# Two transformer layers on one core: where GpSimd pauses, who makes the token weights, and in which order blocks and copies are issued between the router and the expert tiles

## The reference

```python
logits = _gelu(x @ rw1) @ rw2                 # router, 8 experts
probs = jax.nn.softmax(logits, axis=-1)
wgt, idx = jax.lax.top_k(probs, TOP_K)        # TOP_K = 2
for e in range(E):
    Ye = _gelu(x @ w1[e] + b1[e]) @ w2[e] + b2[e]
    Ce = _gelu(b1[e]) @ w2[e] + b2[e]
    for k in range(TOP_K):
        mask = idx[..., k] == e
        active = jnp.any(mask).astype(x.dtype)
        out = out + active * wgt[..., k:k + 1] * jnp.where(mask[..., None], Ye, Ce)
```

## Time and profile before

| what | value |
|---|---|
| three timed runs | 407.2, 411.9, 412.66 us; median 411.9 us |
| the profiled execution | 405.77 us, of which its span is 403.9 us |
| TensorE matmul busy | 315.3 us, 78% of the span |
| VectorE busy | 306.2 us, 76% |
| ScalarE busy | 267.8 us, 66% |
| GpSimd busy | 180.6 us, 45% |
| mean granted TensorE clock | 0.925 of full speed |

### The profile page before, as it was taken

How to read it: one execution, slowest core, us unless ns; L and a number is a source line. 1 busy time by engine, 2 the same in 40 slices (tenths; PEclk the granted TensorE clock), 3 DMA queues, 4 the chain that set the end, 5 groups by cost and what they waited for, 6 DMA issues and landing times.

```text
span 403.9 us, 8728 instructions
## 1 busy us (share of the span) xinstructions
PE 315.3 (78%) x2708; PEld 217.7 (54%) x2709; DVE 306.2 (76%) x745; ACT 267.8 (66%) x540; POOL 180.6 (45%) x245
## 2 busy tenths in 40 slices
PE   0075988989989996878767215798999999999991
PEld 0053327655467654545434114665777777777760
DVE  4998998793875566897989885784787777788760
ACT  1825767634696388889798665661777778777770
POOL 3052305293286058535567459311444455445432
PEclk9998899989999999999979555896999999999997
DMA  5950001943097158431406549445678777777522
GB/s 181 379 238 0 2 0 62 174 110 100 0 148 223 39 71 181 118 108 36 123 15 198 156 108 337 181 178 208 161 247 263 254 230 247 228 218 256 156 27 26
DMA packets 27298, 60.48 MB, mean 150 GB/s; under 512 B 4305, under 2 KB 17954, under 8 KB 24066
## 3 DMA queue, kind: packets, MB, share of 16 engines
q1 hardware_dynamic: 20658, 53.20, 40.5%
q0 software_dynamic: 4416, 6.13, 9.4%
q10 hardware_dynamic: 2192, 0.75, 0.7%
HBM read 29.00 MB, written 6.85 MB: 89 GB/s over the span
## 4 chain that ended last, share of the span: by engine, by line
PE 45%; DVE 29%; ACT 10%; issue 9%; DMA 4%; POOL 1%; ACTq 0%; DVEq 0%; POOLq 0%
PE bank L1270 8%; PE bank L1637 7%; PE bank L1655 7%; PE bank L1640 4%; PE bank L1658 4%; DVE MX L2000 3%; PE bank L1231 2%; DMA STG<-in_l_w_dram 2%; ACT arena L1131 2%; DVE arena L2287 2%; PE bank L1356 2%; DVE stats L1720 2%; PE bank L1382 1%; DVE arena L2292 1%; ACT arena L997 1%
## 5 line engine op out<-in xcount | busy, mean ns | idle before, releaser
L1655 PE MATMUL bank<-arena 128*128 x184 | 63.4, 390 | 2.6 <-DVE X L2274 1.1
L1131 ACT ACTIVATE arena<-arena,B1D 128x128 f32<-128x128 f32 x184 | 57.4, 392 | 8.8 <-DVE arena L2287 8.3
L2287 DVE TENSOR_REDUCE arena<-bank 128x256 f32<-128x512 f32 x92 | 57.3, 681 | 2.5 <-PE bank L1640 2.4
L685 POOL TENSOR_TENSOR W<-STG,W 128x256 f16<-128x256 f32 x64 | 42.7, 700 | 33.2 <-ACT W L882 28.7
L782 POOL DMA_INDIRECT out_dram<-arena,SI x23 | 36.4, 1584 | 36.4 <-DMA out_dram<-arena,SI 19.2
L1658 PE MATMUL bank<-arena 128*128 x184 | 51.2, 279 | 0.0
L685 POOL TENSOR_TENSOR arena<-STG,arena 128x256 f16<-128x256 f32 x56 | 37.5, 705 | 26.4 <-ACT arena L882 24.9
L1637 PE MATMUL bank<-arena 128*128 128x256 f16 x256 | 45.6, 279 | 1.7 <-DVE arena L2250 1.7
L2292 DVE SCALAR_TENSOR_TENSOR arena<-arena 128x512 f16<-128x512 f32 x46 | 29.7, 688 | 22.7 <-ACT arena L1138 22.7
L769 POOL DMA_INDIRECT arena<-token_rows,GI x23 | 22.8, 993 | 51.4 <-ACT WS L1125 43.3
L1640 PE MATMUL bank<-arena 128*128 128x128 f16 x256 | 44.7, 224 | 0.0
(11 more groups left out here) (280 smaller groups left out, 715.1 us busy)
## 6 DMA issues: line engine op xcount, KB each, us to landing
STG<-in_l_w_dram SPq DMA_DIRECT2D x32, 512.0 KB, 4.0
arena<-W SPq DMA_DIRECT2D x16, 1024.0 KB, 4.6
STG<-W SPq DMA_DIRECT2D x7, 1024.0 KB, 5.0
arena<-in_l_w_dram SPq DMA_DIRECT2D x2, 1280.0 KB, 7.3
k_parts<-W SPq DMA_DIRECT2D x2, 768.0 KB, 4.4
arena<-k_parts SPq DMA_DIRECT2D x12, 128.0 KB, 5.2
X<-in_x_dram SPq DMA_DIRECT2D x2, 512.0 KB, 7.4
W<-in_ctx_dram SPq DMA_DIRECT2D x1, 1024.0 KB, 10.2
```

The lines of the kernel that those rows point to most:

```text
L685: ins = nc.gpsimd.tensor_tensor(l, src, h, ALU.subtract)
L1131: ins = nc.scalar.activation(x, x, ACT.Gelu, bias=B1D[:, e, c:c + 1], scale=1.0 / (X_SCALE * W_SCALE))
L1655: nc.tensor.matmul(bank[6 + q][:, :], GDL[:, q, 0, c * P:(c + 1) * P], W2[:, e, c].rearrange("p s d -> p (s d)"), start=(c == 0), stop=Fal ...
L2287: v.tensor_reduce(half, o, AX.X, ALU.add).then_inc(s_dadd, 1)
```

## The change

GpSimd's stretch of low parts for blocks 23 to 25 gets three waits: it goes on only when the first of the last two normalised rows is out (`s_dhs`), after two instructions only when the second router split is done (`s_rhl` 2), after four more only when the third is (`s_rhl` 3). After block 25 it waits for the token weights' scale `RS` and multiplies it out to `DWE` itself; VectorE no longer does. The store of `DWE` gets a semaphore of its own, `s_wrows`, on which only the first gather waits; SP's first `W1` copy waits for the other two stores alone. On ScalarE, scaling block 24 moves ahead of the last `row_high`, the whole of block 25 ahead of the third `router_gelu`, scaling block 26 ahead of the exponentials, and blocks 26's high part and 27 ahead of the store of `DWE`. On SP, the second half of `token_rows` is stored one block load earlier, and the second `W1` copy is issued behind the loads of blocks 30 and 31 instead of ahead of them.

```diff
-            for i in range(25, 28):
+            for i in range(25, 27):
                 load_weights(i)
             store_token_rows(1)
-            for i in range(28, BLOCKS - 2):
+            for i in range(27, BLOCKS - 2):
                 load_weights(i)
...
-            sp.wait_ge(s_rows, 16 * 3)
-            for r in range(2):
-                load_tile_weights(r, r, first=True)
+            sp.wait_ge(s_rows, 32)
+            load_tile_weights(0, 0, first=True)
             for i in range(BLOCKS - 2, BLOCKS):
                 load_weights(i)
+            load_tile_weights(1, 1, first=True)
             sp.wait_ge(s_wlo, BLOCKS - 2)
...
-            def weights_low(i):
+            def weights_low(i, cs=range(HID // D)):
...
-            for i in D_BLOCKS[1:-4]:
+            pool.wait_ge(s_dhs, T - 1)
+            weights_low(D_BLOCKS[1], range(2))
+            pool.wait_ge(s_rhl, 2)
+            weights_low(D_BLOCKS[1], range(2, 4))
+            weights_low(D_BLOCKS[2], range(2))
+            pool.wait_ge(s_rhl, 3)
+            weights_low(D_BLOCKS[2], range(2, 4))
+            weights_low(D_BLOCKS[3])
+            pool.wait_ge(s_dl, 3)
+            nc.gpsimd.tensor_tensor(DWE[:, :, :], PR[:, :, 0:E], RS[:, :].unsqueeze(2).broadcast_to([P, T, E]),
+                                    ALU.mult).then_inc(s_dwe, 1)
+            for i in D_BLOCKS[4:-4]:
                 weights_low(i)
...
-            pool.wait_ge(s_rows, 16 * 3)
+            pool.wait_ge(s_rows, 32)
+            pool.wait_ge(s_wrows, 16)
             pool.wait_ge(s_gi, 1)
...
+            weights_scale(D_BLOCKS[2])
             for t in range(T - 2, T):
                 row_high(t)
-            weights_scale(D_BLOCKS[2])
+            weights_high(D_BLOCKS[2])
             rows_t_out(3)
-            weights_high(D_BLOCKS[2])
-            weights_scale(D_BLOCKS[3])
+            weights_split(D_BLOCKS[3])
             router_gelu(2)
...
+            weights_scale(D_BLOCKS[4])
             act.wait_ge(s_dl, 2)
...
-            weights_high(D_BLOCKS[3])
+            weights_high(D_BLOCKS[4])
+            weights_split(D_BLOCKS[5])
             act.wait_ge(s_dwe, 1)
             act.dma_start(token_rows[:, D:ROW].rearrange("(t p) e -> p t e", p=P),
-                          DWE[:, :, :].bitcast(U32)).then_inc(s_rows, 16)
-            for i in D_BLOCKS[4:-2]:
+                          DWE[:, :, :].bitcast(U32)).then_inc(s_wrows, 16)
+            for i in D_BLOCKS[6:-2]:
                 weights_split(i)
...
-            step(v.tensor_scalar(RS[:, :], DTOPF[:, :, 0], tg[:, 3:4], 1.0 / (G_SCALE * W_SCALE), ALU.mult, ALU.mult))
-            v.tensor_tensor(DWE[:, :, :], PR[:, :, 0:E], RS[:, :].unsqueeze(2).broadcast_to([P, T, E]),
-                            ALU.mult).then_inc(s_dwe, 1)
+            v.tensor_scalar(RS[:, :], DTOPF[:, :, 0], tg[:, 3:4], 1.0 / (G_SCALE * W_SCALE), ALU.mult, ALU.mult
+                            ).then_inc(s_dl, 1)
```

More of the change, by code:

```diff
@@ L409, in flamingo @@
         s_lread = sem("first_router_logits_read")
-        s_dl = sem("router_logits_less_max")
+        s_dl = sem("router_logits_less_max_and_row_scale")
         s_ex = sem("router_exponentials")
@@ L416, in flamingo @@
         s_gbz = sem("gelu_spread_cleared")
-        s_slot = sem("slots_ready")
+        s_wrows = sem("token_weights_stored")
         s_eid = sem("tile_experts_ready")
@@ L676, in _ @@
             estimate_rstd(3, 1)
-            def weights_low(i):
+            def weights_low(i, cs=range(HID // D)):
                 _, hi, lo = weight_block(i)
                 pool.wait_ge(s_whi, i + 1)
-                for c in range(HID // D):
+                for c in cs:
                     src = STG[:, i % 4, c * D:(c + 1) * D]
@@ L685, in weights_low @@
                     ins = nc.gpsimd.tensor_tensor(l, src, h, ALU.subtract)
-                ins.then_inc(s_wlo, 1)
+                if c == HID // D - 1:
+                    ins.then_inc(s_wlo, 1)
             def ones_rows(b):
```

## The result

The changed kernel took 404.2 us in the median of 6 runs (401.71 to 412.36), the kernel before 410.0 in the median of 6 on the same chip: a ratio of 0.9871, 95% interval 0.9825 to 0.9916, so 5.3 us less. (One of the 6 runs, 412.36, lies 2.7% above the fastest and stays out of the ratio.) In the profiled executions it is 401.71 against 405.77 us, spans of 399.9 and 403.9, at a mean granted clock of 0.928 and 0.925.

The account below looks back on a forecast made before the run. Tile 0's start was taken as the bound, set by block 30's load and the gather. An earlier gather landing plus 0.4 from `late_low` gave 4.0 us: 411.9 to 407.9 (span 403.9 to 399.9), range 402.5 to 412.0, chance 0.62.

Parts of the forecast that it names:

- the gather that passes: Rival, chance 0.16: gather passes SP's transfers, landing soon after issue, and tile 0 runs at full clock; gain 7.2, 404.7 us.
- Newton step and third split: VectorE's small instructions no longer slowed beside GpSimd: 1.3 and 0.75 us earlier, less 0.1 lost on ScalarE.
- Token weights' part: VectorE's expert choice: 0.65 saved by moving L2188, 0.6 lost beside GpSimd; `EID` and `GI` 1.9 earlier, bounds 1.4 to 2.5.
- GpSimd's own list: GpSimd's remaining low parts and `DWE` end at 242.6 instead of 246.47, 3.9 us earlier; gather issued at 243.5.
- First copy: SP's first W1 copy, no longer waiting for the weights' store, issued at 240.0 or earlier, 1.9 us sooner.
- Landing of the gather: Tile 0's gather queues behind SP's transfers: lands at 248.0, 249.7 or 251.3; the middle taken, tile 0 3.9 us earlier.
- the last case: At the gather's landing: second W1 copy ahead of the gather, landing at 251.3, tile 0 2.3 us earlier.
- the first case: At the gather's landing: second W1 copy behind the gather, landing at 248.0, tile 0 5.6 us earlier.
- Block 30 out of the way: Block 30 loads behind the first copy only; its ScalarE and VectorE work ends by 249.1, saving 0.4 at tile 0.
- The queue takes it back: Rival, chance 0.16: second copy ahead of the gather, more VectorE waits beside GpSimd; gain 1.4 to 2.3, 410.1 us.
- Slower: Rival, chance 0.06: TensorE's clock stays lower into the tiles, costing 4.8 us over three tiles; 412.7 us.
- The passing case's second half: Within the 0.16 rival of a passing gather: TensorE keeps the clock, so tile 0 goes up 1.6 us faster.

Follow-up runs that it names:

- the repeat: The changed kernel timed once more, nothing altered, beside the kernel with the gather first: median 406.5 us, ratio 0.9886 to the kernel before.
- no_rest: The changed kernel without GpSimd's three waits: ratio 0.9905 to the kernel before.
- rest_only: The kernel before with GpSimd's three waits and nothing else: ratio 0.9983 to the kernel before.
- gather_first: The changed kernel with SP's second W1 copy held back until the first gather has landed: median 401.7 us against 408.5 before, ratio 0.9828.
- the repeats: The changed kernel and the one holding SP's second copy until the gather lands, both timed again on one chip: 406.5 and 404.6 us, ratios 0.9886 and 0.9838.
- copy_only: The kernel before with only the second W1 copy moved behind the loads of blocks 30 and 31: median 407.2 us against 408.5, ratio 0.9866.
- scalar_as_before: The changed kernel with ScalarE's blocks in the order of the kernel before: 403.8 us, read by its events alone.

## Why the prediction was right, and where its steps were off

The time, 404.2, lies in the range, faster by 1.3% where about 1% was forecast. It is 3.7 us under the forecast of 407.9: 1.9 because the kernel before came out at 410.0 in this set and not at 411.9, 1.8 because the medians lie 5.8 apart and not 4.0. It lies nearer the 404.7 of the gather that passes, a case that did not occur, so the time alone would have pointed at the wrong mechanism. The profiled span is the 399.9 us that the sum gave. That agreement is luck: 1.37 of it came ahead of the anchor and 0.49 went again behind tile 0's start. What the passage gave, counted from the anchor, is 30.43 - 27.31 = 3.12 us where the sum has 4.0; the repeat gives 2.78. (The range's ends are 0.2 and 0.1 us off the working given for them, 404.7 - 2 and 410.1 + 2; nothing hangs on it.)

*Newton step and third split*: right. The first of the last two rows began 1.40 after the anchor against 2.72, so 1.32 for 1.3; the third split was done 2.02 earlier, where 1.3 and 0.75 less 0.1 had been counted.

*Token weights' part*: the sign of each piece was right, the sum too careful. L2186 and the cast lost 0.41 and 0.17, together the 0.58 that had been taken as 0.6; but the product (L2201) fell from 0.48 to 0.17, where I had let it stay, since it met GpSimd just ahead of an instruction's end, and the two copies ahead of `GI` went from 1.27 to 0.65, beginning at 240.49 when GpSimd was through its blocks (240.22). The 0.46 that the sum took over from the Newton step was not a fixed price, as the two timelines above show. `EID` came 2.43 earlier instead of 1.9, `GI` 2.77, outside the bound of 2.5. `DWE` on GpSimd took 0.29, at the low end of 0.2 to 0.7.
The Trainium skill, page "SBUF — State Buffer", section "Who interferes with whom", says that an instruction with two SBUF inputs contends with a GpSimd instruction that reads SBUF. The trace agrees for L2186 (0.16 to 0.57), while the subtraction that reads the logits from PSUM beside the same GpSimd work (L2184) stayed at 0.22. The cast, with one SBUF input, and the scale, with one and a column of scalars, were held up too (0.22 to 0.39, and 0.71 against the 0.22 of no_rest).

*GpSimd's own list*: block 27 was done 17.55 after the anchor, where 242.6 is 18.56, 1.0 sooner than taken. The gather was issued where the sum had it (19.52; 243.5 is 19.46), but by luck: `GI` came 0.9 sooner than taken, and 0.95 went between its end and the gather's start, for which the sum had nothing.

*First copy*: mis-sized. It came 2.93 earlier, not 1.9: 0.53 from `EID`, and 0.5 since it had waited 1.44 behind `EID` for the weights' store and now stands 0.94 behind. I had written that the store no longer counts, and put nothing on it. rest_only shows the worth of it: with that wait left in, `EID` earlier by 1.61 moved the copy by 0.96.

*Landing of the gather*, the step that decided: I took the middle of behind, shared and ahead (249.7, that is first copy's issue plus 9.7). It was the last case: issue plus 11.4, as in the kernel before. SP's issue of the second copy began 0.18 us behind the gather's, but the gather's own took 1.22 us, and the copy kept most of the gather's packets back to its end. This step failed by 1.7 us against me; the copy's 1.0 made up part of it, and moving `late_low` out of the way gave 0.2 instead of 0.4. gather_first shows what the first case would have given: tile 0 5.64 earlier than before, and 5.6 had been written for it. Its terms were others: the gather landed 5.67 earlier instead of 5.2, and the 0.4 of `late_low` was not saved, since block 30 was the last wait.

*Block 30 out of the way*: right, 5.6 us earlier on ScalarE, off the chain.

*Rivals.* "The queue takes it back" had the mechanism that ruled, the copy ahead of the gather, at 1.4 to 2.3 us; the passage gave 3.1 since the copy itself came earlier than that sum allowed. "The gather passes" did not occur: the gather landed 6.8 us after its issue, and gather_first shows what held it. "Slower" did not occur either: tile 0 went up at a granted 0.61, as before (0.62), and from 255 to 270 us the clock was 1.00. The passing case's second half, 1.6 us from a tile 0 at full clock (2.4 GHz, against mostly 1.2), was met by chance in gather_first. Busy times by stretch while tile 0 goes up (us; PE, PEld, DVE, ACT, POOL; granted clock; DMA; GB/s), changed kernel, then gather_first:

```profile
249.98:254.17 4.19, 4.19 (x32) 3.45 (x33) 1.84 (x3) 1.90 (x4) 1.74 (x3) 0.61 0.40 130
```

```profile
249.64:252.40 2.76, 2.76 (x34) 2.56 (x35) 1.89 (x3) 1.09 (x1) 2.76 (x6) 1.00 0.85 321
```

The tile went up 1.43 us faster, but from its start to the end of the span only 0.56 of it was left. Counted from tile 0's start, tile 1 went up 1.24 us earlier, but tile 0's way down began only 0.61 earlier: ahead of it TensorE waited 1.34 us for VectorE, against 0.69 in the changed kernel. So more than half of the clock's gain was lost to VectorE there. It is one pair: in the repeats tile 0 took 4.74 and 4.30 us to go up, neither at full clock, and the two rests differ by 0.07.

*What stays open.* The passage gave 3.1 us and, in the repeat, 2.8; the timed ratios give 5.3 and 4.7, with intervals from 3.4 to 7.2 and from 1.7 to 7.6. Both the head ahead of the anchor (222.67 to 229.02 in identical code) and the rest behind tile 0 (147.7 to 150.3) vary by more than that gap. In the rest it goes with a stretch of low granted clock. Stretches with it, kernel before, changed, copy_only (columns as above):

```profile
270.00:285.00 15.00, 13.71 (x86) 8.94 (x83) 9.10 (x19) 4.96 (x14) 2.92 (x3) 0.77 0.50 158
```

```profile
265.00:280.00 15.00, 13.71 (x85) 9.13 (x83) 9.11 (x19) 4.54 (x13) 2.59 (x2) 0.77 0.46 152
```

```profile
270.00:285.00 15.00, 13.71 (x95) 9.46 (x94) 10.19 (x22) 5.70 (x17) 3.58 (x3) 0.89 0.50 159
```

At 0.89 the rest took 147.7, at 0.77 149.4 and 149.9. In copy_only tile 0 went up at full clock besides. scalar_as_before had both as well (0.89 over the same window, 147.9), gather_first the fast tile 0 but 0.77, and took 149.4; so the later stretch is the likelier cause, though no run changes it alone. Whether the change makes the kinder pattern more frequent, or the gap is the noise of few runs, the runs don't tell.

## What to carry to other kernels

Count a small gather's landing from the first transfer that the big queue has outstanding, not from its own issue, and move what isn't needed yet behind it: one wait on SP was worth 2.5 us at tile 0's start here, nearly as much as the whole change (3.1). An earlier result pays only if the wait that stands beside it goes too: resting GpSimd alone brought `EID` forward by 1.6 and tile 0 by 0.4. And compare two traces from an event ahead of the change; here a third of the gain in span had nothing to do with it.

## What the hardware showed that I had not expected

GpSimd began a gather 0.95 us after the end of the row that wrote its indices (241.24 to 242.19), where an instruction queued behind its own list waited 0.19; I had taken the issue to be at the writing. And a gather begun 0.18 us ahead of a 1 MB copy still landed as late as with the copy in front; its own issue lasts 1.22 us. In copy_only and scalar_as_before it began 0.9 us ahead of the copy, still less than that, and landed 10.9 and 12.0 us behind the first copy all the same.
